# Differential attention on one Trainium2 core: the order of score pieces, shared-bank uses and V rounds within a slot

## The chip, the core and the metric

The kernel runs on one core of one Trainium2 chip. The metric is device time in microseconds (us). The engines are named as in the profile: PE is the matrix engine (PEld its weight loads), ACT the scalar engine, DVE the vector engine, POOL the GpSimd engine, SP the engine that issues most DMAs.

## What is computed

The program is a stack of five stages on an input of 16 sequences ("batches") of 512 tokens with 128 features: differential attention, grouped attention, a mixture of experts, eight linear-attention blocks and a ternary feed-forward stage. The change lies in the first stage alone. Cut to what matters, that stage is:

```python
q, k = (x @ Wq.T), (x @ Wk.T)          # each 2 x 8 heads of 8
v = (x @ Wv.T)                         # 8 heads of 16
q, k = rotary(rms_norm(q)), rotary(rms_norm(k))
y1 = causal_attn(q1, k1, v, scale)     # softmax(q k^T * scale, causal) v
y2 = causal_attn(q2, k2, v, scale)
y = (y1 - lambda_full * y2).reshape(B, T, D)
x = x + y @ Wproj.T                    # x is layer-normed ahead of the projections
```

## The kernel before, in words

The stage is the function `diff_attention`. It is written as one hand-ordered program for each engine; the engines meet only at semaphores. There are 16 batches (`NB`), and each has 8 pairs of heads. PE walks through **slots**, one for each pair: slot m of batch b (m from 0 to 7) scores pair n = 8b + m + 1. In the text "slot 3" is m = 3, "the start of slot m" is the first product of its `score_diagonal`, and "batch" is the span of eight slots that begins with m = 0.

**Score pieces.** For a pair, `score_diagonal` (lines 1394 and 1396, into the two banks SX) computes the four blocks on the diagonal, and `score_later` (lines 1408 to 1419, into the three banks SY) the blocks below it. ACT takes the exponential of each with one instruction: `exp_diagonal` (line 1565, SX into PT) and `exp_later` (line 1570, SY into PT). SX and SY are single: `score_diagonal(n)` waits for `probs_x`, the exponential of the diagonal of pair n-1, and `score_later(n)` for `probs_y`, that of its later blocks. POOL masks the diagonal (`mask`, line 1648).

**V rounds.** Two pairs make a group, four groups a batch. `weigh` (line 1431) multiplies PT with V for a group into bank O. An even slot does the rounds `EARLY` of the group before, an odd slot the rounds `DIAG`; each is split in two halves, one ahead of `score_later` and one behind it. The end of `DIAG` raises `av_ready`. DVE then copies O (`copy_o`, line 1819), PE turns the copy (`turn_o0` to `turn_o3`, line 1295) and DVE divides and combines it (`combine`, lines 1825, 1827, 1834); its second instruction raises `o_used`.

**Shared bank uses.** One tile M of two banks serves everything else that PE does: for the batch after this one and the next but one the turned input (`turn_x`, line 1227), the projections of Q and K and their rotated forms (`project_q`, `project_k`, `project_qs`, `project_ks`, lines 1234, 1241, 1249, 1256), the sums of squares (`sum_q`, `sum_k`, lines 1268 to 1279) and `project_v` (line 1288), and for the batch before the turned result and its projection (`turn_y`, line 1333; `project_out`, line 1341). Most slots hold two of them, one ahead of `score_later` and one behind it: slot 0 `project_ks` and `turn_o2`, slot 1 `sum_q`, slot 2 `sum_k` and `turn_o3`, slot 3 `project_v`, slot 4 `turn_y` and `turn_o0`, slot 5 `project_out` and `turn_x`, slot 6 `project_q` and `turn_o1`, slot 7 `project_k` and `project_qs`.

**What these wait for.** `project_v` waits for `o_used` of the group that `turn_o3` turned, that is for `combine(p, 3)`. DVE does that one behind `split_two(c, Q)` (lines 1753, 1758, 1760, 1762), which needs ACT's `rms` of Q (lines 1531, 1534) and POOL's `rotate`. `turn_x` waits for `xn_ready`, that is for `centre` (line 1730). DVE does that one behind `copy_o(b, 0)`, which waits for the end of slot 3's `DIAG`, `split_two(c, K)` and `combine(b, 0)`. `project_out` waits for ACT's `copy_yT` (line 1547) of what `turn_y` turned.

**ACT in a slot.** `exp_diagonal`, then in some slots copies and powers (slot 1 `rms` of Q, slot 2 `rms` of K, slot 4 `copy_v`, slots 6 and 7 `square`), then `exp_later`, then in slot 4 `copy_yT` and in slot 5 `copy_xT`.

DVE's and POOL's orders are fixed by their own programs, `dve_program` and `pool_program`, and SP's by `sp_program`, which loads Q and K for a half batch at a time.

Of the kernel before, what the change touches and what calls it, by code (L numbers as in the profile page):

```python
# [1081 lines left out]
def diff_attention(nc, C, XT, G, NB):  # L1082
# [4 lines left out]
    EARLY = ((1,), (3, 5))  # L1087
    DIAG = ((0, 2), (4, 6))
# [7 lines left out]
    with ExitStack() as ctx:  # L1096
# [84 lines left out]
        probs_y = sem("probs_y")  # L1181
# [34 lines left out]
        def pe_program(pe):  # L1216
# [235 lines left out]
            for b in range(NB + 1):  # L1452
                p, c, c2 = b - 1, b + 1, b + 2
                tail, now, then, next_but_one = b >= 1, b < NB, c < NB, c2 < NB
                for m in range(8):
                    n = 8 * b + m + 1
                    group = 4 * b + m // 2 - 1
                    weighing = 0 <= group < 4 * NB
                    if n < 8 * NB:
                        score_diagonal(n)  # L1460
                    if m == 0 and then:
                        project_ks(c)
                    if m == 1 and then:
                        sum_q(c)
                    if m == 2 and then:
                        sum_k(c)
                    if m == 2 and c == NB:
                        g_sum_k()
                    if m == 4 and tail:
                        turn_y(p)  # L1470
                    if m == 5 and tail:
                        project_out(p)
                    if m == 6 and next_but_one:
                        project_q(c2)
                    if m == 7 and next_but_one:
                        project_k(c2)
                    if m == 6 and c2 == NB:
                        g_project_q()
                    if m == 7 and c2 == NB:
                        g_project_kk()  # L1480
                    if weighing and m % 2 == 0:
                        pe.wait_ge(probs_y, 2 * group + 2)
                        if group:
                            pe.wait_ge(o_copied, group)
                        weigh(group, EARLY[0])
                    if weighing and m % 2 == 1:
                        pe.wait_ge(masked, 2 * group + 2)
                        weigh(group, DIAG[0])
                    if n < 8 * NB:
                        score_later(n)  # L1490
                    if m == 0 and tail:
                        turn_o2(p)
                    if m == 2 and tail:
                        turn_o3(p)
                    if m == 3 and then:
                        project_v(c)
                    if m == 3 and c == NB:
                        g_project_v()
                    if m == 4 and now:
                        turn_o0(b)  # L1500
                    if m == 5 and c2 <= NB:
                        turn_x(c2)
                    if m == 6 and now:
                        turn_o1(b)
                    if m == 7 and next_but_one:
                        project_qs(c2)
                    if m == 7 and c2 == NB:
                        g_project_qs()
                    if weighing and m % 2 == 0:
                        weigh(group, EARLY[1])  # L1510
                    if weighing and m % 2 == 1:
                        weigh(group, DIAG[1]).then_inc(av_ready, 1)

        def act_program(act):
            def copy_xT(c):
                act.wait_ge(xT_filled, c + 1)
                if c:
                    act.wait_ge(v_filled, c)
                act.activation(xnT[:, :], M[:, 0, :], ACT.Copy).then_inc(xT_copied, 1)

            def square(c, x):
                act.wait_ge(filled[x], c + 1)
                if c:
                    act.wait_ge(ss_filled[x], c)
                act.activation(sq[:, x, :], lead(c, 0) if x == K else M[:, 0, :], ACT.Square).then_inc(sq_ready[x], 1)

            def rms(c, x):
                act.wait_ge(ss_filled[x], c + 1)
                if c:
                    act.wait_ge(normed[x], c)  # L1530
                act.activation(rs[:, x, :], lead(c, 2 + x), ACT.Ln, scale=1.0 / HD,
                               bias=C["rms_eps"][:, 0:1]).then_inc(ss_taken[x], 1)
                act.drain()
                act.activation(rs[:, x, :], rs[:, x, :], ACT.Exp, scale=-0.5).then_inc(rs_ready[x], 1)

            def copy_v(c):
                act.wait_ge(v_filled, c + 1)
                act.wait_ge(zeroed, 1)
                if c >= 2:
                    act.wait_ge(av_ready, 4 * (c - 1))  # L1540
                act.activation(V[:, c % 2, :, :, 0:VD].rearrange("p t h d -> p (t h) d"),
                               lead(c, 4).rearrange("p (a d) -> p a d", d=VD), ACT.Copy
                               ).then_inc(v_taken, 1)

            def copy_yT(p):
                act.wait_ge(yT_filled, p + 1)
                act.activation(yT[:, :], M[:, 1, :], ACT.Copy).then_inc(yT_copied, 1)

            def g_copy_sum():
                act.wait_ge(g_k_summed, 1)  # L1550
                act.wait_ge(split[K], NB)
                act.activation(restK, M[0:32, 1, :], ACT.Copy).then_inc(g_sum_copied, 1)

            def g_copy_v():
                act.wait_ge(v_filled, NB + 1)
                act.wait_ge(g_zeroed, 1)
                act.activation(G["v0"][:, :, :, 0:8].rearrange("p t h d -> p (t h) d"),
                               M[:, 0, 0:P].rearrange("p (a d) -> p a d", d=8), ACT.Copy
                               ).then_inc(v_taken, 1)

            def exp_diagonal(n):
                act.wait_ge(x_ready, n + 1)
                if n >= RING:
                    act.wait_ge(av_ready, (n - RING) // 2 + 1)
                act.activation(PT[:, n % RING, :, 0:512], SX[:, :, :], ACT.Exp, scale=SCALE  # L1565
                               ).then_inc(probs_x, 1)

            def exp_later(n):
                act.wait_ge(y_scored, n + 1)
                act.activation(PT[:, n % RING, :, 512:HEAD_COLS],  # L1570
                               SY[:, :, :].rearrange("p a n -> p (a n)").rearrange(
                                   "p (i n) -> p i n", i=2), ACT.Exp, scale=SCALE
                               ).then_inc(probs_y, 1)

            act.preload_act_table_set("natural_log_exp_and_others")
            copy_xT(0)
            square(0, Q)
            square(0, K)
            rms(0, Q)
            rms(0, K)  # L1580
            copy_v(0)
            copy_xT(1)
            square(1, Q)
            exp_diagonal(0)
            exp_later(0)
            square(1, K)
            act.wait_ge(lam_sums, 1)
            act.activation(lam_s[:, 2:4], lam_s[:, 0:2], ACT.Exp).then_inc(lam_exps, 1)
            for b in range(NB + 1):
                p, c, c2 = b - 1, b + 1, b + 2  # L1590
                tail, then, next_but_one = b >= 1, c < NB, c2 < NB
                for m in range(8):
                    n = 8 * b + m + 1
                    if n < 8 * NB:
                        exp_diagonal(n)
                    if m == 1 and then:
                        rms(c, Q)
                    if m == 2 and then:
                        rms(c, K)
                    if m == 3 and c == NB:  # L1600
                        g_copy_sum()
                    if m == 4 and then:
                        copy_v(c)
                    if m == 4 and c == NB:
                        g_copy_v()
                    if m == 6 and next_but_one:
                        square(c2, Q)
                    if m == 7 and next_but_one:
                        square(c2, K)
                    if n < 8 * NB:  # L1610
                        exp_later(n)
                    if m == 4 and tail:
                        copy_yT(p)
                    if m == 5 and c2 <= NB:
                        copy_xT(c2)
# [2245 lines left out]
```

## Time and profile before

| | us |
|---|---|
| median of 3 runs | 3207.44 (3206.28 to 3207.70) |
| span of the profiled execution | 3203.1 |
| PE busy in it | 2943.1 (92%) |
| ACT busy in it | 2325.1 (73%) |
| first `score_diagonal` to the last start of one | 33.0 to 519.8 |

The page's own time for the profiled execution is its span, from the first to the last instruction; the median of the runs is 4.3 us (0.13%) above it, which holds what lies around the span. Times in rows are us from the span's start. In a timeline row the first number is the start, the second the duration (of several instructions merged, from the first start to the last end); what stands in square brackets is how long the engine sat idle before, and what ended that. The end of a matrix product is modelled and overlaps the next start by some hundredths.

### The profile page before, as it was taken

The numbers are of one execution on the slowest core, as the hardware profiler recorded it, in microseconds if no ns is written. First come the engines' busy times: TensorE is split into PE (matmuls) and PEld (weight loads), VectorE is DVE, ScalarE is ACT, GpSimd is POOL, SyncE is SP. The second block draws the span as 40 slices with busy tenths as digits, with TensorE's granted clock in tenths as the row PEclk, the third lists the DMA queues.
The fourth block names the chain that finished last, engine by engine and source line by source line (L and its number), as shares of the span: only waits on it lengthen the run. The fifth ranks groups of instructions, "written<-read, shape, count | busy, mean of one in ns | idle before, by whom it ended". The sixth has DMA issues, their size and how long they took to land. (4 is left out here: it accounts for less than half of the span.)

```text
span 3203.1 us, 66211 instructions
## 1 busy us (share of the span) xinstructions
PE 2943.1 (92%) x22258; PEld 1857.9 (58%) x22258; DVE 2466.5 (77%) x6944; ACT 2325.1 (73%) x3601; POOL 2092.1 (65%) x2402
## 2 busy tenths in 40 slices
PE   6999997788898898789579999999999999999979
PEld 3555554344444444578446666666666666666658
DVE  5666665888787776468468888888888888888867
ACT  5777874465565566544279999999999999999933
POOL 5566664345555563477657887887887887887744
PEclk8999998799898999899879999999999999999989
DMA  4534434222222211386400000000000000000001
GB/s 120 129 101 116 118 96 95 58 62 67 61 53 67 67 48 43 117 280 185 149 15 1 17 1 7 11 6 12 1 17 1 17 1 16 1 13 4 1 14 40
DMA packets 151509, 178.31 MB, mean 56 GB/s; under 512 B 18619, under 2 KB 122784, under 8 KB 151076
## 3 DMA queue, kind: packets, MB, share of 16 engines
q1 hardware_dynamic: 142084, 157.14, 18.9%
q0 software_dynamic: 9088, 16.94, 1.5%
q8 instruction: 179, 2.93, 0.4%
q14 instruction: 158, 1.29, 0.1%
HBM read 99.82 MB, written 75.95 MB: 55 GB/s over the span
## 5 line engine op out<-in xcount | busy, mean ns | idle before, releaser
L3372 PE MATMUL lb_FF<-lb_h,lb_w 128*128 128x512 f32 x1024 | 501.2, 592 | 0.0
L3601 DVE TENSOR_SCALAR lb_z<-lb_M,lb_mv,lb_rstd 128x128 f32<-128x128 f32 x1024 | 344.9, 399 | 3.3 <-POOL lb_rstd L3526 3.0
L3489 ACT ACTIVATE lb_h<-lb_H,lb_prm 128x512 f32<-128x512 f32 x512 | 326.6, 697 | 2.6 <-PE lb_H L3363 2.6
L3526 POOL TENSOR_TENSOR lb_rstd<-lb_rstd,half 128x4 f32<-128x4 f32 x256 | 260.4, 1017 | 37.2 <-issue 1.3
L3357 PE MATMUL lb_H<-lb_x1s,lb_w 128*128 128x512 f32 x512 | 272.2, 532 | 0.8 <-issue 0.8
L3372 PEld LDWEIGHTS lb_FF<-lb_h,lb_w 128*128 128x128 f32 x1024 | 193.5, 189 | 89.5 <-issue 61.0
L544 ACT ACTIVATE ga_PT<-ga_S 128x384 f32<-128x384 f32 x256 | 111.7, 489 | 183.2 <-PE ga_S L355 183.2
L1570 ACT ACTIVATE da_PT<-da_SY 128x1536 f32<-128x1536 f32 x128 | 185.2, 1447 | 72.2 <-PE da_SY L1419 72.0
L3593 DVE BATCH_NORM_STATS2 lb_stats<-lb_M 128x6 f32<-128x128 f32 x1024 | 227.2, 284 | 13.1 <-PE lb_M L3316 7.9
L1648 POOL TENSOR_SCALAR_AFFINE_SELECT da_PT<-da_PT 128x1024 f32<-128x1024 f32 x128 | 141.4, 1110 | 132.4 <-ACT da_PT L1565 132.4
L3358 PE MATMUL lb_H<-lb_x1s,lb_w 128*128 128x512 f32 x512 | 203.0, 397 | 0.0
L3363 PE MATMUL lb_H<-lb_x1s,lb_w 128*128 128x512 f32 x512 | 202.8, 397 | 0.1
L1431 PE MATMUL da_O<-da_PT,da_V 128*32 128x128 f32 (+2 forms) x3584 | 191.4, 325 | 2.6 <-DVE da_oT L1819 2.1
L3544 POOL CAST lb_x1s<-lb_x 128x512 fp32r<-128x512 f32 x128 | 78.0, 609 | 174.3 <-DVE lb_x L3626 174.3
L2623 POOL DMA_INDIRECT moe_ys<-moe_y,moe_dest x156 | 157.3, 1009 | 50.5 <-issue 45.5
L3537 POOL TENSOR_TENSOR lb_xs<-H,lb_xs 128x512 fp32r<-128x512 f32 x126 | 167.5, 1329 | 18.1
L3547 POOL TENSOR_TENSOR lb_x1s<-lb_x,lb_x1s 128x512 fp32r<-128x512 f32 x128 | 163.4, 1276 | 20.9 <-issue 20.9
L3558 POOL TENSOR_TENSOR lb_y<-lb_ao,H 128x512 f32<-128x512 f32 x128 | 165.2, 1291 | 16.7 <-ACT lb_ao L3476 14.6
L795 DVE TENSOR_REDUCE ga_bm<-ga_S 128x8 f32<-128x1024 f32 x128 | 156.2, 1220 | 24.7 <-PE ga_S L379 22.2
L792 DVE TENSOR_REDUCE ga_bm<-ga_S 128x8 f32<-128x1024 f32 x128 | 156.1, 1220 | 18.9 <-PE ga_S L379 16.9
L3470 ACT ACT_TABLE_LOAD x131 | 168.1, 1283 | 2.4
L3570 POOL TENSOR_TENSOR lb_y<-lb_ff,lb_x 128x512 f32<-128x512 f32 x128 | 164.9, 1288 | 7.4 <-PE lb_M L3316 4.9
(514 smaller groups left out, 8851.9 us busy)
## 6 DMA issues: line engine op xcount, KB each, us to landing
moe_w<-experts_dram SPq DMA_DIRECT2D x39, 384.0 KB, 3.3
da_qT<-da_stq SPq DMA_DIRECT2D x64, 192.0 KB, 4.0
da_kT<-da_stk SPq DMA_DIRECT2D x64, 192.0 KB, 3.6
moe_x<-moe_xs SPq DMA_DIRECT2D x39, 260.0 KB, 3.7
tc_g<-moe_ys SPq DMA_DIRECT2D x32, 256.0 KB, 4.3
ga_q<-ga_stq SPq DMA_DIRECT2D x20, 384.0 KB, 6.1
lb_split<-moe_parts SPq DMA_DIRECT2D x8, 896.0 KB, 6.5
da_stq<-da_parts SPq DMA_DIRECT2D x16, 384.0 KB, 2.4
```

The lines of the kernel that those rows point to most:

```text
L1431: last = pe.matmul(O[32 * c:32 * c + 32, q0:q0 + cols], V[:, (n // 4) % 2, j, 2 * (n % 4) + c % 2, :], PT[:, (2 * n + c // 2) % RING, c % ...
L1570: act.activation(PT[:, n % RING, :, 512:HEAD_COLS], SY[:, :, :].rearrange("p a n -> p (a n)").rearrange("p (i n) -> p i n", i=2), ACT.Exp, ...
L3357: pe.matmul(H[:, k % 2, :], w1[:, 0, k, :], x1s[:, 0, :], start=True, stop=False)
L3358: pe.matmul(H[:, k % 2, :], w1[:, 1, k, :], x1s[:, 0, :], start=False, stop=False)
L3363: pe.matmul(H[:, k % 2, :], w1[:, 0, k, :], x1s[:, 1, :], start=False, stop=True).then_inc(h_filled, 1)
L3372: pe.matmul(FF[:, :], w2[:, k, :], h[:, k, :], start=(k == 0), stop=(k == KC - 1)).then_inc(ff_filled, 1)
L3470: act.preload_act_table_set("gelu_apprx_tanh_and_others")
L3489: act.activation(h[:, k, :], H[:, k % 2, :], ACT.Gelu_apprx_tanh, bias=col(FB1 + k, i)).then_inc(h_ready, 1)
L3526: pool.tensor_tensor(out[:, :], out[:, :], C["half"][:, 0:NT], ALU.pow).then_inc(done, 1)
L3537: pool.tensor_tensor(part_of_x(i, 1), state(i), part_of_x(i, 0).bitcast(F32), ALU.subtract).then_inc(xs_ready, 1)
L3593: v.bn_stats(stats[:, t, :], M[:, t * P:(t + 1) * P])
L3601: last = v.tensor_scalar(z[:, t, :], M[:, t * P:(t + 1) * P], mv[:, t, 0:1], rstd[:, t:t + 1], ALU.subtract, ALU.mult)
```

## The change

On PE a slot now runs `score_diagonal(n)`, `score_later(n)`, then both uses of the shared bank in the order that they had, then both halves of the V rounds with their waits. In slot 0 `turn_o2` still follows `project_ks`; in slot 7 `project_k` stands directly ahead of `project_qs`. On ACT `rms` of Q and of K move from ahead of `exp_later` to behind it in their slots 1 and 2, and `copy_v` moves from slot 4, ahead of `exp_later`, to slot 3, behind it. `square` stays ahead of `exp_later`. No instruction is added or removed, and the programs of DVE, POOL and SP are the same.

```diff
                     if n < 8 * NB:
                         score_diagonal(n)
+                        score_later(n)
                     if m == 0 and then:
                         project_ks(c)
+                    if m == 0 and tail:
+                        turn_o2(p)
                     if m == 1 and then:
                         sum_q(c)
                     if m == 2 and then:
                         sum_k(c)
                     if m == 2 and c == NB:
                         g_sum_k()
-                    if m == 4 and tail:
-                        turn_y(p)
-                    if m == 5 and tail:
-                        project_out(p)
-                    if m == 6 and next_but_one:
-                        project_q(c2)
-                    if m == 7 and next_but_one:
-                        project_k(c2)
...
-                    if weighing and m % 2 == 0:
-                        pe.wait_ge(probs_y, 2 * group + 2)
-                        if group:
-                            pe.wait_ge(o_copied, group)
-                        weigh(group, EARLY[0])
-                    if weighing and m % 2 == 1:
-                        pe.wait_ge(masked, 2 * group + 2)
-                        weigh(group, DIAG[0])
-                    if n < 8 * NB:
-                        score_later(n)
-                    if m == 0 and tail:
-                        turn_o2(p)
                     if m == 2 and tail:
                         turn_o3(p)
                     if m == 3 and then:
                         project_v(c)
...
+                    if m == 4 and tail:
+                        turn_y(p)
                     if m == 4 and now:
                         turn_o0(b)
+                    if m == 5 and tail:
+                        project_out(p)
                     if m == 5 and c2 <= NB:
                         turn_x(c2)
+                    if m == 6 and next_but_one:
+                        project_q(c2)
...
                     if m == 6 and now:
                         turn_o1(b)
                     if m == 7 and next_but_one:
+                        project_k(c2)
                         project_qs(c2)
...
                     if weighing and m % 2 == 0:
-                        weigh(group, EARLY[1])
+                        pe.wait_ge(probs_y, 2 * group + 2)
+                        if group:
+                            pe.wait_ge(o_copied, group)
+                        weigh(group, EARLY[0] + EARLY[1])
                     if weighing and m % 2 == 1:
-                        weigh(group, DIAG[1]).then_inc(av_ready, 1)
+                        pe.wait_ge(masked, 2 * group + 2)
+                        weigh(group, DIAG[0] + DIAG[1]).then_inc(av_ready, 1)
...
                     if n < 8 * NB:
                         exp_diagonal(n)
-                    if m == 1 and then:
-                        rms(c, Q)
-                    if m == 2 and then:
-                        rms(c, K)
                     if m == 3 and c == NB:
                         g_copy_sum()
-                    if m == 4 and then:
-                        copy_v(c)
-                    if m == 4 and c == NB:
-                        g_copy_v()
...
                     if n < 8 * NB:
                         exp_later(n)
+                    if m == 1 and then:
+                        rms(c, Q)
+                    if m == 2 and then:
+                        rms(c, K)
+                    if m == 3 and then:
+                        copy_v(c)
+                    if m == 3 and c == NB:
+                        g_copy_v()
```

## Rows read from the trace of the kernel before

**Rows 1.** Window of batch 9: length; busy PE, PEld, DVE, ACT, POOL; PEclk; DMA:

```profile
314.81:345.55 30.74, 29.52 (x392) 15.81 (x390) 20.16 (x41) 24.21 (x25) 18.97 (x19) 1.00 0.44 113
```

**Rows 2.** PE's groups by line, 69.2 to 468.2 us (batches 1 to 13):

```profile
L1408 PE MATMUL da_SY<-da_qT,da_kT 48*128 48x256 bf16 x104 | 29.1, 280 | 4.5 <-ACT da_PT L1570 4.5
...
L1341 PE MATMUL da_M<-da_wout,da_yT 128*128 128x128 f32 x104 | 15.1, 288 | 4.2 <-ACT da_yT L1547 4.2
...
L1227 PE MATMUL da_M<-ident,da_xn 128*128 128x128 f32 x52 | 8.5, 287 | 7.5 <-DVE da_xn L1730 7.5
```

**Rows 3.** PE's timeline through batch 9, from slot 0 to slot 6:

```profile
314.82 0.23 PE L1394 MATMUL da_SX<-da_qT,da_kT 48*128 48x128 bf16 x1
...
315.14 1.13 PE L1256 MATMUL da_M<-da_xnT,da_w 128*128 128x512 f32 x2
...
318.12 0.86 PE L1431 MATMUL da_O<-da_PT,da_V 128*32 128x256 f32 x16
318.91 0.23 PE L1394 MATMUL da_SX<-da_qT,da_kT 48*128 48x128 bf16 x1
...
326.60 0.28 PE L1408 MATMUL da_SY<-da_qT,da_kT 48*128 48x256 bf16 x1 [0.32 <-ACT da_PT L1570]
...
327.15 1.16 PE L1288 MATMUL da_M<-da_w,da_xnT 128*128 128x128 f32 x8
...
328.81 0.23 PE L1394 MATMUL da_SX<-da_qT,da_kT 48*128 48x128 bf16 x1
...
336.07 0.66 PE L1227 MATMUL da_M<-ident,da_xn 128*128 128x128 f32 x4 [0.57 <-DVE da_xn L1730]
336.66 0.65 PE L1431 MATMUL da_O<-da_PT,da_V 128*32 128x128 f32 x16
337.23 0.23 PE L1394 MATMUL da_SX<-da_qT,da_kT 48*128 48x128 bf16 x1
```

**Rows 4.** ACT's timeline in slot 1 of batch 9:

```profile
319.35 1.03 ACT L1565 ACTIVATE da_PT<-da_SX 128x1024 f32<-128x1024 f32 x1 [0.26 <-PE da_SX L1396]
...
321.57 1.43 ACT L1570 ACTIVATE da_PT<-da_SY 128x1536 f32<-128x1536 f32 x1
```

**Rows 5.** DVE's and POOL's timelines in batch 9:

```profile
321.90 1.11 POOL L1648 TENSOR_SCALAR_AFFINE_SELECT da_PT<-da_PT 128x1024 f32<-128x1024 f32 x1
...
322.34 1.21 DVE L1753 TENSOR_TENSOR da_rotA<-da_rotA,da_rs 128x512 f32<-128x512 f32 x1
...
324.93 1.38 DVE L1762 CAST da_parts<-da_rotB 128x512 bf16<-128x512 f32 x1
...
324.93 1.10 POOL L1648 TENSOR_SCALAR_AFFINE_SELECT da_PT<-da_PT 128x1024 f32<-128x1024 f32 x1
...
326.54 0.42 DVE L1827 TENSOR_TENSOR da_u<-da_M,da_rsum 128x256 f32<-128x256 f32 x1
...
331.61 0.43 DVE L1762 CAST da_parts<-da_rotB 128x512 bf16<-128x512 f32 x1
...
333.57 2.44 DVE L1730 TENSOR_SCALAR da_xn<-XT,da_mv,da_rstd 128x128 f32<-128x128 f32 x4
```

**Rows 6.** PE's timeline where pieces stand beside their like (last batch, first batch):

```profile
522.54 1.73 PE L1431 MATMUL da_O<-da_PT,da_V 128*32 128x256 f32 x48
...
39.60 0.28 PE L1408 MATMUL da_SY<-da_qT,da_kT 48*128 48x256 bf16 x1
...
40.38 0.50 PE L1268 MATMUL da_M<-da_sqs,da_heads 128*128 128x512 f32 x1
```

**Rows 7.** Batch 0: PE's timeline in slots 5 to 7, and the window after the wait:

```profile
58.32 0.66 PE L1227 MATMUL da_M<-ident,da_xn 128*128 128x128 f32 x4 [2.05 <-DVE da_xn L1730]
...
59.73 0.29 PE L1394 MATMUL da_SX<-da_qT,da_kT 48*128 48x128 bf16 x1
...
65.11 0.23 PE L1394 MATMUL da_SX<-da_qT,da_kT 48*128 48x128 bf16 x1
...
59.20:62.50 3.30, 3.30 (x30) 1.19 (x22) 0.69 (x1) 1.56 (x3) 1.03 (x1) 0.50 1.01 200
```

More of the change, by code:

```diff
@@ L1468, in pe_program @@
                         g_sum_k()
-                    if m == 4 and tail:
-                        turn_y(p)
-                    if m == 5 and tail:
-                        project_out(p)
-                    if m == 6 and next_but_one:
-                        project_q(c2)
-                    if m == 7 and next_but_one:
-                        project_k(c2)
[L1477 to L1480, printed above, removed]
-                    if weighing and m % 2 == 0:
-                        pe.wait_ge(probs_y, 2 * group + 2)
-                        if group:
-                            pe.wait_ge(o_copied, group)
-                        weigh(group, EARLY[0])
-                    if weighing and m % 2 == 1:
-                        pe.wait_ge(masked, 2 * group + 2)
-                        weigh(group, DIAG[0])
-                    if n < 8 * NB:
-                        score_later(n)
-                    if m == 0 and tail:
-                        turn_o2(p)
                     if m == 2 and tail:
@@ L1498, in pe_program @@
                         g_project_v()
+                    if m == 4 and tail:
+                        turn_y(p)
                     if m == 4 and now:
                         turn_o0(b)
+                    if m == 5 and tail:
+                        project_out(p)
                     if m == 5 and c2 <= NB:
                         turn_x(c2)
+                    if m == 6 and next_but_one:
+                        project_q(c2)
+                    if m == 6 and c2 == NB:
+                        g_project_q()
                     if m == 6 and now:
@@ L1505, in pe_program @@
                     if m == 7 and next_but_one:
+                        project_k(c2)
                         project_qs(c2)
                     if m == 7 and c2 == NB:
+                        g_project_kk()
                         g_project_qs()
                     if weighing and m % 2 == 0:
-                        weigh(group, EARLY[1])
+                        pe.wait_ge(probs_y, 2 * group + 2)
+                        if group:
+                            pe.wait_ge(o_copied, group)
+                        weigh(group, EARLY[0] + EARLY[1])
                     if weighing and m % 2 == 1:
-                        weigh(group, DIAG[1]).then_inc(av_ready, 1)
+                        pe.wait_ge(masked, 2 * group + 2)
+                        weigh(group, DIAG[0] + DIAG[1]).then_inc(av_ready, 1)
         def act_program(act):
```

## The prediction

> **What bounds the kernel now.** I read the busy time by windows first. Over one batch of the first stage PE is busy for 29.52 of 30.74 us, at granted clock 1.00, and the next engine, ACT, for 24.21 [rows 1]. PE is nearly full, so a new order can win at most its idle time. PE's groups by line say where that is: in batches 1 to 13, which take 399 us or 30.7 each, PE sat idle 7.5 us ahead of `turn_x`, 4.5 ahead of `score_later` and 4.2 ahead of `project_out` [rows 2]. That is 16.2 us, 1.25 a batch, 0.5% of the kernel.
>
> PE's timeline then shows that full and free to move are two things. Two stretches of a batch are chains over other engines, and PE only fills time beside them [rows 3].
>
> The first runs from the start of slot 0 to `project_v`. `project_v` starts at 12.33 us (327.15 less 314.82) behind a `score_later` that waited 0.32 for ACT. But it could not have come much earlier: the `combine` instruction that it waits for ends at 326.96, 12.14 us after the start of slot 0 [rows 3, 5]. That one stands on DVE behind `split_two` of Q, and two of its four instructions ran beside a mask of POOL and took longer. The product began 0.67 us before the mask of 321.90 ended and took 1.21; the last cast began with the next mask and took 1.38, ending 0.28 after it. In the same batch's `split_two` of K that cast took 0.43 (331.61).
>
> The second runs from the end of slot 3 to `turn_x`: DVE's copy of O, `split_two` of K, `combine` and `centre`, the last at 333.57 for 2.44 us, ending 336.01; `turn_x` starts at 336.07 [rows 3, 5]. From the start of slot 4 (328.81) that is 7.26 us, whatever PE does meanwhile.
>
> So a batch is: start of slot 0 to `project_v` 12.33, to slot 4 1.66, to `turn_x` 7.26, to slot 6 1.16, slots 6 and 7 8.32 (to 345.55); sum 30.73 [rows 1, 3].
>
> **The change, part by part.** No instruction is added or removed, so I price places and neighbours. The profiled execution has span 3203.1 us, the median of the runs is 3207.44; I add the differences to the median.
>
> *Fewer changes of kind on PE.* Diagonal and later pieces apart cost 0.33 (314.82 to 315.14) and 0.55 (326.60 to 327.15), 0.88 together [rows 3]; where a `score_later` is followed at once by a `score_diagonal`, both take 0.78 (39.60 to 40.38) [rows 6]. Saves 0.10 a slot. The V rounds: an `EARLY` half takes 0.79 (318.12 to 318.91), a `DIAG` half 0.57 (336.66 to 337.23) [rows 3]. One `EARLY` and two `DIAG` halves in a row, 48 products, take 1.73 busy, of which 0.07 overlaps the next start (as 0.86 against 0.79): 1.66 against 1.93 apart, 0.13 saved for each seam closed [rows 3, 6]. Two uses of the shared bank in a row: no row at full clock that I use shows it; bounds 0 and 0.20. I take 0.12, between the two prices above. Slots 6 and 7 together save twice 0.35: 0.70.
>
> *Start of slot 0 to `project_v`.* ACT's `rms` of Q now follows the later exponential. Slot 1 begins at 4.09 less 0.35, 3.74. The diagonal exponential starts 0.44 after that and takes 1.03, the later one 1.43, `rms` 1.19 (the gap between 320.38 and 321.57) [rows 3, 4]: done at 7.83. Before, DVE's product started at 7.52 but was held until the mask ended at 8.19 (323.01) [rows 5]. POOL's order is untouched and begins with the mask behind slot 0's diagonal exponential, whose place does not move. So the product is still held by the same mask, the cast by the next, and `combine` still ends at 12.14. `project_v` starts 0.06 later (the distance from 336.01 to 336.07), at 12.20: saves 0.13. PE is there at about 10.5 (12.33 less the wait of 0.32, seams of 1.0 in slots 0 to 3 and slot 3's first `DIAG` half, 0.57), or some tenths later where ACT holds it up: it waits some 1.5 us. The waits of `score_later` for ACT in slots 2 and 3 are hidden by this one.
>
> *Behind `project_v`.* Both `DIAG` halves now stand between it and `av_ready`: 1.01 (twice 0.57 less 0.13) where 0.57 stood. Costs 0.44, and DVE's copy of O, `turn_o0`, `centre` and `turn_x` are all that much later.
>
> *Slots 4 and 5.* `turn_y` and `turn_o0` come earlier, but DVE's chain starts with the end of slot 3, so the 7.26 stays. `copy_v` is done behind slot 3's later exponential, in time for `turn_o0`. `copy_yT` has a whole V round to hide in: `project_out` loses its wait of 0.32. But that only moves it to `turn_x`. In 7.26 us PE now works 6.37 (less 0.32 and 0.57 of wait), minus the first `DIAG` half of slot 5 (0.57), minus seams of 0.58 (0.35 in slot 4, and 0.10 and 0.13 around slot 5): about 5.2. **The wait ahead of `turn_x` grows from 0.57 to about 2.0 us.** Behind it stand both `DIAG` halves instead of one: 0.44 again.
>
> *Sum.* -0.13 + 0.44 + 0.44 - 0.70 = +0.05 a batch, +0.7 us over 13. For batch 0 and the three passes at the end I take nothing; bounds -4 and +3, a wait or two of 1 us each.
>
> *The clock.* One row shows a wait of that length: in batch 0 PE sat idle for 2.05 us ahead of `turn_x`, and from 59.2 to 62.5 us the granted clock was 0.50, the lower level [rows 7]. Slot 6 of that batch took 5.38 us (59.73 to 65.11); slot 0 of batch 9, with a like load, 4.09 [rows 3, 7]. A fall costs 1.29, and slots 6 and 7 have no cover. With 0.57 the clock stayed at 1.00 [rows 1, 3]. The number of falls is bounded by 0 and 13, 0 to 16.8 us. One row cannot say that every such wait brings one; I take 7, 9.0 us.
>
> Total 3207.4 + 0.7 + 9.0 = 3217 us.
>
> **The rivals.** *The clock holds (no change).* If a wait of 2.0 us seldom brings a fall (none to four), the time is 3208 to 3213. For it: the order costs almost nothing by itself, and the row of batch 0 comes from a batch that had waited more often before. Against: place and length are the same.
>
> *The ports decide otherwise (faster).* DVE's last cast and POOL's mask of 324.93 start in the same hundredth, and the mask wins [rows 5]. If in the new order the cast starts first, it takes 0.43 as at 331.61, `combine` ends 0.95 earlier and `project_v` with it, as PE is there 1.5 us early. It decides as soon as the cast leads by some hundredths: 13 times -0.95, -12.4 us, 3196 with no fall and 3205 with seven. The Trainium skill (SBUF — State Buffer, "SBUF: two separate sides") calls the port pair of DVE and GpSimd an exclusive lock that whoever starts first holds for the whole instruction. By that rule so close a start could turn either way; the trace agrees on the blocking (1.38) and shows one order only. Against it: the product is released by the mask's end, and what follows on both engines is counted from there, as before.
>
> *More falls (slower still).* If every batch has one, +16.8; and if the new wait of 1.5 us ahead of `project_v` brings some too, 4 of them at 1.29 add 5: 3225 to 3230. For it: that wait stands close behind short ones of `score_later`. Against: no row shows a fall after a wait under 2 us.
>
> **How the numbers follow.** 0.2% is 6.4 us, about what a measurement of this kernel can tell from no change. The forecast with five to nine falls (3214 to 3220) has a chance of 0.45, the clock that holds 0.30, the ports 0.13, more falls 0.12. Faster by 0.2% (under 3201): 0.10 of the ports' case and 0.02 of the clock that holds, 0.12. Slower by 0.2% (over 3213.9): 0.52, 0.41 of the forecast (all but its lower edge) and 0.11 of more falls. The rest, 0.36, is no change. The range reaches from 3202, where the clock holds and the ends gain, to 3230, every batch falling and both unknown prices at their worse ends; it leaves out most of the ports' case and the worst of the last. The likeliest case's own range is 3212 to 3222.
>
> **What would show it.** In the profile of the changed kernel: `turn_x` sits idle for about 2 us a batch on DVE's `centre`, 25 us and more over 13 batches; `project_out` no longer on ACT; `project_v` waits about 1.5 us on DVE's line 1827; the cast of 324.93's kind still takes near 1.4; slots 6 and 7 take 3.7 to 3.8 us each at full clock; and the granted clock over the first stage shows falls to 0.50 behind the waits. Wrong would be: batches of under 30 us (the chains were not what binds), casts of 0.43 beside the masks, a stage at clock 1.00 with the 2 us waits in it, or slots 6 and 7 still at 4.1 (no seam was worth anything; that alone would be +0.7 a batch, 9 us).

## The result and the profile after

The changed kernel takes 3221.74 us (median of 7 runs, 3213.91 to 3228.17) against 3207.44 before (median of 7 runs): ratio 1.0046, 95% interval 1.0031 to 1.0060. It is slower by some 14 us. The profiled execution of it has a span of 3217.9 us and took 3219.66.

Where the time went is read in the same views as before. First the windows of the changed kernel: one batch that shows nothing special (batch 2), one that does (batch 4), and batches 1 to 13 together.

```profile
98.42:128.97 30.55, 26.95 (x392) 16.72 (x388) 20.51 (x41) 23.89 (x26) 18.94 (x19) 1.00 0.45 113
160.79:193.85 33.06, 29.81 (x392) 18.71 (x388) 20.51 (x41) 24.00 (x26) 18.94 (x19) 0.90 0.42 105
67.90:480.80 412.90, 367.13 (x5048) 228.56 (x5044) 266.78 (x533) 310.82 (x326) 246.25 (x235) 0.95 0.42 109
```

The same 392 products keep PE busy for 26.95 us in batch 2, where they took 29.52 of 30.74 before [rows 1]. PE has 2.6 us less to do, yet the batch is hardly shorter: 30.55. In batch 4 the granted clock averages 0.90, and the batch takes 33.06. Batches 1 to 13 took 399 us before; now they take 413.

The groups of PE by line over those 13 batches show what it waits for:

```profile
L1408 PE MATMUL da_SY<-da_qT,da_kT 48*128 48x256 bf16 x104 | 29.5, 283 | 0.7
...
L1288 PE MATMUL da_M<-da_w,da_xnT 128*128 128x128 f32 x104 | 16.4, 305 | 19.0 <-DVE da_u L1820 19.0
...
L1341 PE MATMUL da_M<-da_wout,da_yT 128*128 128x128 f32 x104 | 15.1, 288 | 0.0
...
L1227 PE MATMUL da_M<-ident,da_xn 128*128 128x128 f32 x52 | 10.7, 340 | 26.1 <-DVE da_xn L1723 26.1
```

Against [rows 2], the wait of `project_out` for ACT is gone (4.2 to 0) and that of `score_later` nearly (4.5 to 0.7). The wait of `turn_x` for `centre` has grown from 7.5 to 26.1 us, 2.0 a batch, and `project_v` has a new one of 19.0, 1.5 a batch. Idle time on PE went from 16 to 46 us. The mean of one `turn_x` product also grew, from 287 to 340 ns: some of them ran at the lower clock.

PE's timeline through batch 2, which had the full clock:

```profile
98.42 0.23 PE L1394 MATMUL da_SX<-da_qT,da_kT 48*128 48x128 bf16 x1
...
110.60 1.16 PE L1288 MATMUL da_M<-da_w,da_xnT 128*128 128x128 f32 x8 [1.45 <-DVE da_u L1820]
112.71 0.23 PE L1394 MATMUL da_SX<-da_qT,da_kT 48*128 48x128 bf16 x1
...
119.97 0.66 PE L1227 MATMUL da_M<-ident,da_xn 128*128 128x128 f32 x4 [2.10 <-DVE da_xn L1723]
121.57 0.23 PE L1394 MATMUL da_SX<-da_qT,da_kT 48*128 48x128 bf16 x1
...
125.27 0.23 PE L1394 MATMUL da_SX<-da_qT,da_kT 48*128 48x128 bf16 x1
...
128.97 0.23 PE L1394 MATMUL da_SX<-da_qT,da_kT 48*128 48x128 bf16 x1
```

From the start of slot 0, `project_v` starts at 12.18 us, slot 4 at 14.29, `turn_x` at 21.55, slot 6 at 23.15, and slots 6 and 7 take 3.70 each. The answers to these in [rows 3] are 12.33, 13.99, 21.25, 22.41 and 8.32 for both.

DVE's and POOL's timelines in the same batch, beside [rows 5]:

```profile
105.51 1.09 POOL L1641 TENSOR_SCALAR_AFFINE_SELECT da_PT<-da_PT 128x1024 f32<-128x1024 f32 x1
...
106.33 0.81 DVE L1746 TENSOR_TENSOR da_rotA<-da_rotA,da_rs 128x512 f32<-128x512 f32 x1 [0.92 <-ACT da_rs L1527]
...
108.51 1.37 DVE L1755 CAST da_parts<-da_rotB 128x512 bf16<-128x512 f32 x1
...
108.51 1.10 POOL L1641 TENSOR_SCALAR_AFFINE_SELECT da_PT<-da_PT 128x1024 f32<-128x1024 f32 x1
...
110.12 0.42 DVE L1820 TENSOR_TENSOR da_u<-da_M,da_rsum 128x256 f32<-128x256 f32 x1
```

DVE's product now waits for ACT's powers and starts at 7.91 us from slot 0 instead of 7.52. It ends at 8.72, where it ended at 8.73 before: it is released with the end of the same mask. The cast and the next mask again start in the same hundredth, the cast takes 1.37, and `combine` ends at 12.12. The chain to `project_v` has not moved.

Last, the clock. PE's timeline at the waits of batches 9 and 4:

```profile
341.47 1.11 PE L1227 MATMUL da_M<-ident,da_xn 128*128 128x128 f32 x4 [2.11 <-DVE da_xn L1723]
...
344.38 0.23 PE L1394 MATMUL da_SX<-da_qT,da_kT 48*128 48x128 bf16 x1
...
172.97 1.40 PE L1288 MATMUL da_M<-da_w,da_xnT 128*128 128x128 f32 x8 [1.45 <-DVE da_u L1820]
```

and two windows, one that begins within the first wait, 0.42 us ahead of `turn_x`, and one behind the second (PEclk is the third number from the end):

```profile
341.05:344.35 3.30, 2.88 (x36) 2.10 (x36) 0.96 (x3) 0.60 (x1) 0.00 (x0) 0.50 0.69 189
...
173.80:177.10 3.30, 3.30 (x48) 2.42 (x48) 0.80 (x2) 1.47 (x3) 0.79 (x1) 0.50 0.64 243
```

In batch 9 the four transposes of `turn_x` took 1.11 us, not 0.66, and slot 6 began 2.91 us after `turn_x` instead of 1.60. Of the 13 batches, seven have a fall to 0.50 that begins in `turn_x`'s wait or less than 1 us behind it (3, 4, 6, 8, 9, 11, 12), and four have one so behind `project_v`'s (4, 7, 10, 11); the second fall of batch 11 lasts twice as long as any other. Four batches have none and take 30.55 to 30.57 us. Before, none of the 13 had a fall.

So: without falls 13 batches would take 397.3 us (an estimate, 13 times 30.56), 1.7 less than the 399 before; the falls add 15.7 (413.0 less 397.3). That is the loss; outside these batches the two spans differ by 0.8 us.

### The profile page after: what moved, and what is told of

Read it like the earlier page. It is cut to its first block and busy times, and to the rows that moved or that the text cites. A ratio compares the mean times of both kernels' runs of the same rounds, so it can differ in the third digit from the quotient of the medians.

```text
span 3217.9 us, 66211 instructions
## 1 busy us (share of the span) xinstructions
PE 2922.2 (91%) x22258; PEld 1884.2 (59%) x22258; DVE 2472.9 (77%) x6944; ACT 2321.2 (72%) x3601; POOL 2093.8 (65%) x2402
## 3 DMA queue, kind: packets, MB, share of 16 engines
q14 instruction: 158, 1.29, 0.1%
## 5 line engine op out<-in xcount | busy, mean ns | idle before, releaser
L1558 ACT ACTIVATE da_PT<-da_SX 128x1024 f32<-128x1024 f32 x128 | 130.7, 1021 | 76.6 <-PE da_SX L1396 76.6
L1431 PE MATMUL da_O<-da_PT,da_V 128*32 128x128 f32 (+2 forms) x3584 | 175.7, 338 | 0.0
```

Of the source, the lines that this page charges most:

```text
L1431: last = pe.matmul(O[32 * c:32 * c + 32, q0:q0 + cols], V[:, (n // 4) % 2, j, 2 * (n % 4) + c % 2, :], PT[:, (2 * n + c // 2) % RING, c % ...
```

## The experiments

All kernels were timed in five rounds against the kernel before, whose median in these runs was 3205.85 us (first four kernels) and 3205.28 (last four). Ratios are to it. Falls and waits are counted in one profiled execution of each kernel. In these executions the span less batches 1 to 13 lies anywhere from 2794.8 to 2810.3 us, so a difference of a few us between two kernels is read in the batches and not in the span. Two theories stood at first: the loss is the **clock**, which falls behind the waits on PE; or it is the **order itself**, that is the work now put behind `project_v` and `turn_x`.

### Filling the waits with work that changes nothing

```diff
             def project_out(p):
...
+                for twice in range(2):
                     for t in range(NT):
                         last = pe.matmul(M[:, 1, t * P:(t + 1) * P], yT[:, t * P:(t + 1) * P], wout[:, :],
...
             def turn_o(b, g):
...
+                for again in range(3 if g == 3 else 1):
                     for t in range(NT):
                         last = pe.transpose(M[:, 0 if g in (0, 3) else 1, t * P:(t + 1) * P],
```

> The changed kernel, with its two waits on PE partly filled by work that changes nothing: project_out's products are issued twice, turn_o3's transposes three times (each writes the same values again). Theory A (the loss is the granted clock falling behind the waits): the chains over POOL and DVE are untouched, so a batch without a fall stays at 30.5 to 30.6 us, PE's waits shrink from 2.1 to 1.2 us ahead of turn_x and from 1.5 to 0.7 ahead of project_v, the granted clock stays at 1.00 from batch 1 to 13, and the time falls back to 3202 to 3208 although PE does some 1.8 us more a batch. Theory B (the loss is the order itself: both V halves behind project_v and behind turn_x): the time stays at 3216 to 3228 or rises.

Measured: 3204.14 us, ratio 0.9998 (0.9985 to 1.0011). The window over batches 1 to 13:

```profile
69.40:466.70 397.30, 370.95 (x5256) 240.29 (x5252) 266.85 (x533) 310.57 (x326) 246.49 (x235) 1.00 0.44 113
```

and PE's groups by line in it:

```profile
L1288 PE MATMUL da_M<-da_w,da_xnT 128*128 128x128 f32 x104 | 15.1, 288 | 10.5 <-DVE da_u L1822 10.5
L1227 PE MATMUL da_M<-ident,da_xn 128*128 128x128 f32 x52 | 8.5, 287 | 15.7 <-DVE da_xn L1725 15.7
```

PE does more, 5256 products instead of 5048, and all that the change cost is won back: the 13 batches take some 397 us, as estimated above. The clock is 1.00 throughout, every batch takes 30.56 to 30.58 us, and the waits are 1.2 and 0.8 us a batch. `project_v` and `turn_x` still start at 12.2 and 21.56. The places of the chains are those of the changed kernel; only the clock differs. That settles the first question: the loss is the clock, and the waits bring its falls.

### Each half of the change alone

PE's new order with ACT's old one, and the reverse; each is the diff of the change, one engine's part of it.

> PE's new order with ACT's order of before (powers and copy of V ahead of the later exponential). Theory A (PE's order brings the waits, ACT's order hardly matters): score_later of slots 2 and 3 waits longer for ACT, project_v moves from 12.2 to about 12.5 us after the start of slot 0, batches without a fall 30.6 to 31.0 us, falls as in the changed kernel or more, 3218 to 3232. Rival (moving ACT's copies behind its exponentials is what costs): back to 3204 to 3210.

Measured: 3213.99 us, ratio 1.0025 (1.0014 to 1.0036). PE's waits in 69 to 480 us (line waited for: us, times, longest):

```profile
PE da_SY L1408 <- ACT da_PT L1563: 25.4, 22, 1.5
PE da_M L1227 <- DVE da_xn L1723: 17.4, 13, 1.3
PE da_M L1295 <- ACT da_V L1534: 7.5, 13, 0.6
```

`score_later` waits for ACT as expected and `project_v` comes at 12.70 us; most batches without a fall take 31.1, a little over what was expected, and there are fewer falls than expected, five, so the time lies below the range. Four of the five stand behind a new wait of `score_later` of 1.49 us in slot 2 (batches 3, 6, 12 and 13), one behind `turn_x`'s, here 1.34 us (batch 4). `turn_o0` waits 0.6 for `copy_v`: ACT's part of the change removes a wait that PE's part would make.

> PE's order of before with ACT's new order. Theory A: the powers of Q come about 1 us later in slot 1, close behind the mask that held DVE's product before; project_v stays near 12.3 us, batches at 30.6 to 30.9, no falls, 3205 to 3212. Rival (ACT's order is what costs): 3216 to 3228.

Measured: 3215.21 us, ratio 1.0028 (1.0018 to 1.0038). This missed: ACT's order does cost when it stands alone, as the rival had it, but by a wait that the changed kernel doesn't have. ACT's and PE's timelines in slots 1 and 2:

```profile
105.87 1.45 ACT L1570 ACTIVATE da_PT<-da_SY 128x1536 f32<-128x1536 f32 x1 [0.76 <-PE da_SY L1419]
107.21 0.68 ACT L1531 ACTIVATE da_rs<-da_M,rms_eps 128x512 f32<-128x512 f32 x1
...
107.95 0.50 PE L1278 MATMUL da_M<-da_sqs,da_heads 128*128 128x512 f32 x1 [1.21 <-ACT da_rs L1531]
```

In PE's old order `sum_k` stands right behind slot 2's diagonal pieces, and it waits until ACT has read the sum of Q from the bank. Behind the later exponential that read comes late, and PE stands for 1.21 us; `project_v` moves to 13.22 and the batches take 31.55 us (one 31.74), without a fall. So each half alone costs, and the two halves cancel these waits of each other's: together their batches take 30.56 without a fall. What is left together is two longer waits, and more falls.

### V rounds ahead of the uses that wait

Slot 3's and slot 5's V rounds go ahead of `project_v` and of `turn_x`; then each of the two alone.

```diff
+                    if weighing and m == 3:
+                        pe.wait_ge(masked, 2 * group + 2)
+                        weigh(group, DIAG[0] + DIAG[1]).then_inc(av_ready, 1)
                     if m == 3 and then:
                         project_v(c)
...
+                    if weighing and m == 5:
+                        pe.wait_ge(masked, 2 * group + 2)
+                        weigh(group, DIAG[0] + DIAG[1]).then_inc(av_ready, 1)
                     if m == 5 and c2 <= NB:
                         turn_x(c2)
...
-                    if weighing and m % 2 == 1:
+                    if weighing and m % 2 == 1 and m not in (3, 5):
```

> The changed kernel, with the V rounds of slot 3 ahead of project_v and those of slot 5 ahead of turn_x, so that they fill the two waits. Theory A (two chains over DVE set the batch, and what stands behind their ends is paid in full): slot 3's V rounds end before 12 us, DVE's copy starts when combine of the group before is done, at about 12.8 instead of 14.4; turn_x at about 19.9 instead of 21.5; what stands behind turn_x is 1.0 less: batches of 27.8 to 28.3 us, PE nearly full, no falls, 3165 to 3180. Rival (PE's own work or ACT is the bound and the chains are not): batches of 30 us and more, 3200 to 3222.

Measured: 3165.22 us, ratio 0.9871 (0.9850 to 0.9892). The window of batch 2:

```profile
94.25:122.44 28.19, 27.09 (x392) 16.72 (x389) 20.64 (x41) 23.67 (x26) 18.96 (x19) 1.00 0.46 123
```

and PE's waits in 69 to 480 us:

```profile
PE da_M L1227 <- DVE da_xn L1729: 7.2, 12, 0.6
PE da_M L1288 <- DVE da_u L1826: 5.4, 12, 0.5
```

Most batches take 28.20 us, PE is busy for 27.09 of them, and there is no fall from batch 1 to 13. `project_v` is at 12.2 as always; `turn_x` comes at 20.2 (19.9 expected), 1.35 earlier than in the changed kernel, because DVE's chain starts with V rounds that no longer wait for `project_v`: its copy of O begins 12.79 us after the start of slot 0, right behind `combine`, and not at 14.42.

> The changed kernel, with slot 5's V rounds ahead of turn_x (slot 3 as in the changed kernel). Theory A: the wait ahead of turn_x falls from 2.1 to about 1.1 us and brings no more falls; 0.45 less stands behind turn_x: batches of 30.1 us; falls stay only behind the wait of 1.5 us ahead of project_v, three to six of about 1 us: 3199 to 3208. Rival (falls come from something other than the two waits): seven or more falls, 3208 to 3218.

Measured: 3198.30 us, ratio 0.9987 (0.9974 to 1.0001). The time lies 0.7 us below the range expected, and the number of falls, three to six expected, is twelve. PE's timeline at the wait ahead of `project_v` in batch 2:

```profile
111.23 1.59 PE L1288 MATMUL da_M<-da_w,da_xnT 128*128 128x128 f32 x8 [1.45 <-DVE da_u L1823]
```

and the window behind it:

```profile
111.90:115.10 3.20, 3.20 (x47) 2.50 (x47) 0.35 (x1) 1.34 (x2) 0.95 (x1) 0.50 0.64 246
```

The one batch without a fall takes 29.54 us, less than the 30.1 expected, as all 1.0 us of the V rounds that filled the wait left the path behind `turn_x`. But 12 of 13 batches have a fall behind `project_v`, where the changed kernel has four with the same wait of 1.45 us. No fall stands behind `turn_x`, whose wait is now 0.3 to 1.1 us. Batches 1 to 13 of this execution take 399.1 us, no less than before the change; that the time is 7 us below the kernel before is not explained by them.

> The changed kernel, with slot 3's V rounds ahead of project_v (slot 5 as in the changed kernel). Theory A: project_v stays at 12.2 us with a wait of some 0.4; DVE's copy of O starts behind combine at about 13.1, turn_x at 20.2 instead of 21.5 and with a wait of about 1.8 us: batches of 29.2 us, falls behind turn_x in some, 3182 to 3196. Rival (the chain to turn_x hangs on project_v and not on the end of slot 3's V rounds): turn_x stays at 21.5, 3204 to 3222.

Measured: 3193.87 us, ratio 0.9972 (0.9961 to 0.9984). `turn_x` starts at 20.2 us in every batch, so in the changed kernel its chain hung on the end of slot 3's V rounds. Batches without a fall take 29.2. PE's waits:

```profile
PE da_M L1227 <- DVE da_xn L1726: 20.9, 13, 1.6
PE da_M L1288 <- DVE da_u L1823: 5.8, 13, 0.5
```

Six of the 13 waits of 1.6 us bring a fall, which costs 1.4 to 1.5 us each; those of 0.5 none.

### The cast that a mask holds

POOL's third part of Q goes ahead of slot 2's mask, so that this mask cannot run beside DVE's last cast.

```diff
+                    if m == 2 and c <= NB:
+                        third(c, Q)
                     if n < 8 * NB:
                         mask(n)
...
-                    if m == 2 and c <= NB:
-                        third(c, Q)
                     if m == 3 and c < NB:
                         third(c, K)
```

> The changed kernel, with POOL's third part of Q ahead of slot 2's mask, so that no mask runs beside DVE's last cast. Theory A (the cast held by the mask sets project_v): the cast takes 0.43 instead of 1.38, project_v comes at 11.2 to 11.3 us instead of 12.2 and with a wait of about 0.5 that brings no falls; batches without a fall 29.6 us, falls behind turn_x as before: 3200 to 3210. Rival (the hold is covered: PE or ACT could not use the 0.95 us): project_v stays near 12, 3215 to 3225.

Measured: 3204.01 us, ratio 1.0000 (0.9990 to 1.0010). DVE's and POOL's timelines in batch 2:

```profile
109.30 0.43 DVE L1755 CAST da_parts<-da_rotB 128x512 bf16<-128x512 f32 x1
...
109.81 1.16 POOL L1634 TENSOR_TENSOR da_parts<-da_rotB,da_parts 128x512 bf16<-128x512 f32 x1 [0.49 <-DVE da_parts L1755]
```

and PE's waits in 69 to 480 us:

```profile
PE da_M L1227 <- DVE da_xn L1723: 26.3, 13, 2.1
PE da_M L1288 <- DVE da_u L1820: 7.2, 14, 0.6
```

The cast takes 0.43, `project_v` comes at 11.24 and the batches without a fall take 29.62 us, 0.94 less. The waits of 0.5 ahead of `project_v` bring no falls; those of 2.0 to 2.1 ahead of `turn_x` bring them in ten of 13 batches. The hold of the cast is real and lies on the path in the changed kernel.

> Both V rounds ahead of the waiting uses, and POOL's third part of Q ahead of slot 2's mask. Theory A: project_v is then bound by PE itself (11.7 us), batches of 27.7 us instead of 28.2, no falls: 3155 to 3163, faster than either of the two kernels by 1.3% or more. Rival (POOL's later mask holds up the V rounds of slot 5): batches of 28.2 us or more, 3165 or more.

Measured: 3165.44 us, ratio 0.9873 (0.9853 to 0.9893), no different from the V rounds moved alone. PE's waits:

```profile
PE da_M L1227 <- DVE da_xn L1729: 5.1, 13, 0.5
```

`project_v` is at 11.67 as expected, but the batch takes 27.98, not 27.7. In the kernel with the V rounds alone, one batch (9) happened to have a cast of 0.43 with the mask in its old place: `project_v` stood at 11.67 there too, and the batch took 27.75. POOL's and DVE's timelines, first in batch 2 of this kernel, then in that batch 9:

```profile
106.11 1.16 POOL L1647 TENSOR_SCALAR_AFFINE_SELECT da_PT<-da_PT 128x1024 f32<-128x1024 f32 x1
106.82 0.98 DVE L1752 TENSOR_TENSOR da_rotA<-da_rotA,da_rs 128x512 f32<-128x512 f32 x1
...
304.93 1.19 POOL L1640 TENSOR_TENSOR da_parts<-da_rotB,da_parts 128x512 bf16<-128x512 f32 x1
305.88 0.79 DVE L1752 TENSOR_TENSOR da_rotA<-da_rotA,da_rs 128x512 f32<-128x512 f32 x1
```

DVE's product of K ends 0.53 and 0.55 us behind the instruction of POOL that it ran beside. The mask, now behind the third part, ends 12.88 us after the start of slot 0, where the third part ended at 12.65; the product, and with it `centre` and `turn_x` (19.98 against 19.75), come 0.23 later. So the rival had a point: the later mask does hold something up, DVE's product of K and not the V rounds of slot 5. What is left is 0.22 us a batch, some 3 us, too little to tell in these runs.

## Why the prediction was right, point by point

The prediction said 3217 us, in 3202 to 3230, and slower; 3221.7 was measured, and its mechanism is the one that happened. Eleven falls came, more than the five to nine of the forecast (3214 to 3220), and four of them were of the kind that the rival of more falls named.

*Two chains set the batch.* Right: `project_v` at 12.20 forecast and 12.18 to 12.20 measured; slot 4 at 14.30 and 14.29; `turn_x` at 21.56 and 21.55. Both chains were then moved on their own: the first by the cast (to 11.24), the second by slot 3's V rounds (to 20.2).

*Seams.* Slots 6 and 7 together were to save 0.70 and saved 0.83 against the 8.24 that two slots of 4.09 and 4.15 take in a batch of 30.66 before, or 0.91 against batch 9. The term was a little small, and no run separates its parts; the order alone saves 0.13 us a batch, where the forecast had it cost 0.05.

*The waits.* About 2.0 us ahead of `turn_x` forecast, 2.1 measured; some 1.5 ahead of `project_v`, 1.45 measured; none left ahead of `project_out`.

*The clock.* Seven falls of 1.29 us forecast behind `turn_x`; seven came in the profiled execution, and the five among them that were alone in their batch (3, 6, 8, 9 and 12) cost 1.26 to 1.49. That it was just seven is luck: the number was half of a bound, and in the kernel with the cast freed it was ten. The term that was mis-sized is the falls behind `project_v`: the forecast had none, and left four of them to the rival of more falls. They came, at 1.0 us each where they were alone in their batch (7 and 10), some 4 us of the 15.7 that all falls cost, where 9.0 were forecast. That is 6.7 more; the order cost 2.4 less than forecast. The net of 4.3 is nearly all of the 4.7 between forecast and result.

*ACT's part* was priced at nothing, with the mask as its cover. In the new order that holds (the product ends at 8.72 against 8.73). What the text did not see is that ACT's new order is only free because `sum_k` moved away too: alone it costs 0.9 us a batch.

*The rivals.* The clock did not hold. The ports decided as before in all 13 batches; where POOL's third part went first, the cast took 0.43 and the batch was 0.94 us shorter, so the price of 0.95 was right. In one batch with the V rounds moved (batch 9) the cast took 0.43 without that, and the batch was 0.45 us shorter: there PE's own work set `project_v`.

## What to carry to other kernels

When an in-order engine is nearly full, ask of each reordering what it puts **behind** the wait that ends last, and not only how much it saves: here 2.6 us of PE work a batch were saved, and 2.4 of them turned into waits, because V rounds that could have run during the waits stood behind them. Put the work that can already run ahead of the use that waits for another engine; the same pieces in that order made the kernel 1.3% faster than before. And a longer single wait on PE can cost more than its length: price the granted clock behind it from rows.

## What the runs showed that I had not expected

In batches 1 to 13, waits of 1.45 us brought falls of the clock too: four times in 13 batches in the changed kernel, 12 times in 13 with slot 5's V rounds moved, at the same wait and the same place. With PE's order alone, waits of 1.34 us did in one of 13 and waits of 1.49 in four. Waits of 1.6 us did in six of 13, waits of 2.0 to 2.1 us in seven and ten of 13, waits of up to 1.2 us in none. What decides for a given wait stays open; no run here was made to tell. And useless work can pay: with 208 more products in batches 1 to 13 the ratio to the kernel before went from 1.0046 to 0.9998.
